# A four-layer stack on one core: order of loads, bias rows and sums in its first stage

## The reference, cut to what matters

```python
x = x + L0_xattn(layernorm(x), ctx, W, b)     # the first stage
x = x + L0_ffn(layernorm(x), Wg, W1, W2, W3)  # 8 experts, each takes its 512 best rows
x = x + L1_xattn(layernorm(x), ctx, ctx, mask, W_out)
x = x + L1_ffn(layernorm(x), w_gate, w_up, w_down)

def L0_xattn(x1, x2, W, b):
    W1, W2 = W[:, :256], W[:, 256:]
    part1 = einsum('bld,ed->ble', x1, W1)
    part2 = einsum('bld,ed->be', x2, W2) / 154
    return part1 + part2[:, None, :] + b

def layernorm(x):
    return (x - mean(x)) / sqrt(var(x) + 1e-5)
```

## Time and profile before

| what | value |
|---|---|
| median of 3 executions | 898.93 us (898.59 to 900.31) |
| the profiled execution, its own time | 899.15 us |
| its span in the trace | 897.4 us |
| first stage (this block) | 0 to about 78.5 us |
| busy in the whole span: PE / DVE / ACT / POOL | 688.7 / 684.1 / 499.9 / 210.8 us |
| granted TensorE clock, mean | 0.87 of full |

### The profile page before, as it was taken

How to read it: one execution, slowest core, us unless ns; L and a number is a source line. 1 busy time by engine, 2 the same in 40 slices (tenths; PEclk the granted TensorE clock), 3 DMA queues, 4 the chain that set the end, 5 groups by cost and what they waited for, 6 DMA issues and landing times.

```text
span 897.4 us, 11482 instructions
## 1 busy us (share of the span) xinstructions
PE 688.7 (77%) x3995; PEld 529.0 (59%) x3995; DVE 684.1 (76%) x1379; ACT 499.9 (56%) x624; POOL 210.8 (23%) x169
## 2 busy tenths in 40 slices
PE   4794227399999954899999999987999995002998
PEld 3573215388988842446665666556887873002998
DVE  5798782378667728999878786887888999997564
ACT  1031010354334432668688786765556997995873
POOL 4621500426656743210111101002430000000000
PEclk9897555599999995899999999998999997555999
DMA  9445620335563456001003100012311732101343
GB/s 325 172 151 187 213 86 3 106 108 124 125 185 60 62 100 222 1 1 43 25 1 128 33 24 25 8 41 95 141 47 37 247 138 93 47 0 47 95 132 104
DMA packets 59491, 84.89 MB, mean 95 GB/s; under 512 B 7984, under 2 KB 47536, under 8 KB 57904
## 3 DMA queue, kind: packets, MB, share of 16 engines
q1 hardware_dynamic: 50176, 61.30, 20.6%
q0 software_dynamic: 7872, 21.11, 9.7%
q10 hardware_dynamic: 1392, 1.82, 0.6%
HBM read 53.68 MB, written 30.54 MB: 94 GB/s over the span
## 4 chain that ended last, share of the span: by engine, by line
PE 45%; DVE 17%; ACT 7%; issue 5%; POOL 4%; DMA 3%; DVEq 0%; ACTq 0%; POOLq 0%
PE bank L1888 8%; PE bank L1844 7%; PE bank L2077 5%; PE bank L2089 4%; PE bank L1313 4%; PE bank L1347 3%; DVE peak L1617 3%; PE bank L1403 3%; PE bank L1370 3%; PE bank L1367 3%; PE bank L1328 2%; POOL x_dram L1934 2%; ACT wgateT L1779 2%; DVE qx L1120 2%; DMA x_dram<-wdownT,idx 1%
## 5 line engine op out<-in xcount | busy, mean ns | idle before, releaser
L1209 ACT ACTIVATE x<-bank,bic 128x512 f32<-128x512 f32 x160 | 105.6, 691 | 38.0 <-PE bank L1347 35.5
L1120 DVE TENSOR_REDUCE qx<-bank 128x4 fp32r<-128x616 f32 x128 | 98.1, 796 | 23.4 <-PE bank L1313 21.8
L1844 PE MATMUL bank<-ux,uwh 128*128 128x512 f32 x384 | 98.5, 395 | 2.6 <-ACT ux L1745 2.4
L1844 PEld LDWEIGHTS bank<-ux,uwh 128*128 128x128 f32 x384 | 71.8, 190 | 20.7 <-issue 3.5
L1347 PE MATMUL bank<-qT,K 128*128 128x512 f32 x128 | 62.6, 500 | 4.2 <-ACT x L1209 1.7
L1313 PE MATMUL bank<-Kb,qTb 128*128 128x308 bf16 x256 | 56.3, 313 | 7.4 <-DVE qx L1120 3.0
L2038 ACT ACTIVATE wgateT<-bank 128x512 f32<-128x512 f32 x32 | 19.1, 597 | 72.8 <-PE bank L2077 72.2
L1834 PE MATMUL bank<-cst,amax 128*1 128x128 f32 x6 | 1.6, 329 | 70.3 <-DVE amax L1589 70.3
L2077 PE MATMUL bank<-xh,wh 128*128 128x512 f32 x128 | 50.8, 397 | 4.7 <-DVE xl L1956 4.7
L1844 PE MATMUL bank<-ux,uwl 128*128 128x512 f32 x192 | 52.2, 394 | 0.0
L2077 PE MATMUL bank<-xh,wl 128*128 128x512 f32 x128 | 50.5, 394 | 0.0
(11 more groups left out here) (352 smaller groups left out, 2023.8 us busy)
## 6 DMA issues: line engine op xcount, KB each, us to landing
xs_dram<-ux POOLq DMA_DIRECT2D x6, 1024.0 KB, 4.2
ux<-xs_dram POOLq DMA_DIRECT2D x6, 1024.0 KB, 5.6
x_dram<-x SPq DMA_DIRECT2D x4, 1024.0 KB, 5.3
xr<-in_w1T SPq DMA_DIRECT2D x8, 512.0 KB, 3.8
xr<-in_w3T SPq DMA_DIRECT2D x8, 512.0 KB, 4.7
xr<-in_w2T SPq DMA_DIRECT2D x8, 512.0 KB, 6.5
row_dram<-xn SPq DMA_DIRECT2D x8, 512.0 KB, 3.1
xr<-x_dram SPq DMA_DIRECT2D x8, 512.0 KB, 7.5
```

The source lines that it names most:

```text
L1120: dve.tensor_reduce(qx[:, k, g * GH:(g + 1) * GH, MROW].rearrange("p (u h) -> p u h", u=2), pair[i][:].rearrange("p (u x) -> p u x", u=2)[ ...
L1209: act.activation(pr[g % 2][h], S_[u % 2], ACT.Exp, bias=bic[:, s // 2, h // GH:h // GH + 1]).then_inc(p_done, 1)
L1844: mm = pe.matmul(bank[j][:, m * TB:(m + 1) * TB], w[:, c * HI + cols:c * HI + cols + P], x[:, part, c * TB:(c + 1) * TB], start=(w is uwh ...
```

## The change

- SyncE waits for w2_in (wx2T and b have landed) behind `rows(1)`, before all other loads. The mask goes ahead of `rows(3)`, the keys' load ahead of step 4's transposed rows, and step 5's ahead of `rows(4)`.
- ScalarE makes all context sums before the first root, and scales the keys at s = 3 and 4.
- VectorE makes the bias rows of batches 1 to 3 at u = 1 directly behind the additions, and the key remainders at u = 10 and 11.
- GpSimd waits before the bias rows of steps 1, 3, 5 and 7 until the first tile of x1 of the step before is added (s_x1 of 1, 9, 17, 25).
- TensorE makes the bias products of batches 1 to 3 directly behind times_w1(2).

```diff
                     rows(1)
+                    sp.wait_ge(w2_in, 32)
                     turned_rows(1)
                     rows(2)
                     turned_rows(2)
                     turned_rows(3)
-                    rows(3)
                     sp.dma_start(mrow[:], ...)
                     sp.dma_start(mcol[:], a["mcol"]).then_inc(g_mk, 16)
                     sp.dma_start(sel[:], a["sel"]).then_inc(g_mk, 16)
+                    rows(3)
+                    key_loads(sp, raw0, 0)
                     turned_rows(4)
+                    turned_rows(5)
                     rows(4)
-                    turned_rows(5)
                     stored(0)
                     turned_rows(6)
-                    key_loads(sp, raw0, 0)
                     turned_rows(7)
...
                     context_sum(0)
-                    rooted(0)
                     act.wait_ge(ctx_in, 16)
                     for b in range(1, B):
                         context_sum(b)
+                    rooted(0)
...
-                        if s in (4, 5):
+                        if s in (3, 4):
                             act.wait_ge(k_set, 3)
                             act.wait_ge(g_mask, 8)
-                            key_heads(act, raw0, K0, Kr0, 0, s - 4)
+                            key_heads(act, raw0, K0, Kr0, 0, s - 3)
...
                         added(u, 1)
+                        if u == 1:
+                            dve.wait_ge(s_sums, SUM_BIAS + B - 1)
+                            for i in range(1, B):
+                                bias_sum(i)
...
                             refined(b)
-                        if u == 1:
-                            dve.wait_ge(s_sums, SUM_BIAS + B - 1)
-                            for i in range(1, B):
-                                bias_sum(i)
...
-                        if u in (11, 13):
-                            key_remainders(dve, raw0, K0, Kr0, 0, u // 2 - 5)
+                        if u in (10, 11):
+                            key_remainders(dve, raw0, K0, Kr0, 0, u - 10)
...
                     for s in range(1, NS):
+                        if s % 2:
+                            pool.wait_ge(s_x1, UT * 2 * (s - 1) + 1)
                         pool.wait_ge(x_in[part_of(s)], 16)
                         biased_rows(s * STEP, (s + 1) * STEP)
...
                     times_w1(2)
+                    for b in range(1, B):
+                        biased(b)
                     for s in range(1, NS + 1):
...
                         x1_turn(s - 1)
-                        if s == 1:
-                            for b in range(1, B):
-                                biased(b)
```

## The result

| | before | changed |
|---|---|---|
| median | 899.62 us (898.59 to 900.31, 4 executions) | 884.75 us (884.69 to 886.27, 4 executions) |
| ratio | | 0.984, 95% interval 0.9823 to 0.9857 |
| profiled execution, its time / span | 899.15 / 897.4 us | 886.27 / 884.5 us |
| next stage starts | 79.01 us | 65.88 us |
| from there to the end of the span | 818.4 us | 818.6 us |

The next stage starts where SyncE issues that stage's first load. The kernel is faster by 14.9 us between the medians and by 12.9 between the two profiled executions; the first stage is 13.1 us shorter. The forecast was 885.6 us, a gain of 13.35.

A forecast was written before the change was run, and what follows sets the result against it. In the first stage, VectorE's small operations with two SBUF inputs were taken to wait for running GpSimd instructions. Terms -14.05 + 0.7 = -13.35 us gave 885.6 us against the 898.93 median; range 883.2 to 889.4.

The forecast's parts named there:

- Loads held: First stage's load queue: SP waits for w2_in, b_bc lands at 9.4 us against 11.6; -2.2 us for TensorE.
- Bias products early: TensorE, behind the third times_w1: bias rows 1 to 3 start at 20.7, not 28.00; -7.3 us, 2.2 from the landing.
- Context sums first: ScalarE's accumulating copies before the first root: sums end at 14, root wanted at 15.1; cost 0.
- GpSimd held: VectorE's batch 1 chain at u=2 and 3 runs undisturbed: 12.21 us becomes 3.67, -8.5 us.
- Keys earlier: VectorE: second key remainders (1.78 us) now also lie before u=12, which starts at 52.6.
- TensorE at the end: Last transposes at 59.1 against 73.15, -14.05 us; closing variance then waits for GpSimd's key mask, +0.7.
- 1: Rival: b_bc's landing not earlier, or held loads or context late; +2.2, 887.8 us; chance 0.17.
- 2: Rival: VectorE's masks or u=2's chain meet a GpSimd add and wait out its rest; 888.1 us; chance 0.08.
- 3: Rival: TensorE's clock dips after an idle gap, costing some 1.6 us; 887.4 us; chance 0.08.
- 4: Rival: the lock isn't the cause, VectorE's chain stays slow with GpSimd idle; 894.3 us; chance 0.03.
- 5: Rival: slower, TensorE at the 1.2 GHz level from first to last transposes; 912.7 us; chance 0.03.
- 6: Rival: no change, what was gained is waited away in the next stage; chance 0.01.

The follow-up runs named there:

- e3: Changed kernel without the load queue's wait for w2_in: 887.23 us, ratio 0.9883.
- e4: Changed kernel with bias products 1 to 3 back behind the first transposes of x1: 890.6 us, ratio 0.9914.
- e9: Changed kernel with the statistics of tiles 0 and 1 again ahead of the bias rows at u=1: 884.85 us, ratio 0.9851.
- e11: Changed kernel with the first root again ahead of the context sums of batches 1 to 3: 885.39 us, ratio 0.9858.
- e1: Kernel before the change plus only GpSimd's waits on the first x1 tile: 891.03 us, ratio 0.9917.
- e2: Changed kernel without GpSimd's waits: 893.09 us, ratio 0.9937.
- e6: Changed kernel with the key steps back at u=11 and 13 (ScalarE's at s=4 and 5): 887.53 us, ratio 0.9872.
- e7: Changed kernel with GpSimd's adds for tiles 20 to 27 released by the mask step, beside VectorE's one-input operations: 889.04 us, ratio 0.9903.
- e5: Changed kernel without GpSimd's waits and with its adds cut to one tile an instruction: 890.45 us, ratio 0.9915.
- e10: e9 with GpSimd's add for tiles 28 to 31 released by the last key remainders instead of u=12: 885.93 us, ratio 0.9866.
- e8: e9 with mask loads ahead of x, mask steps in VectorE's idle start, and GpSimd's last add released by the last key remainders: 885.12 us, ratio 0.9863.

## Why the prediction was right

The time, 884.75 us, lies 0.85 under the forecast, and the steps held one by one:

- Loads held: first bias product at 9.62, forecast 9.4, and e3 gives the hold 1.9 us for the 2.2 of the sum. The rows for tiles 8 to 15 came at 17.55, with a wait of 0.65 us that the slack took.
- Bias products early: 20.70 for 20.7; without the move (e4) 23.42. The +0.7 for the statistics was there (u=2 at 23.67 for 23.7), and e9 shows that it needn't be paid.
- Context sums first: priced at nothing, and e11 says nothing. They ended at 13.97, forecast 14.
- GpSimd held: -8.5 forecast, 3.67 us in u=2 and 3 as said; e1 shows the hold alone as sufficient for it, and e2 that without the hold the stalls stay. This is the largest term. In e2 it is worth 9.8 us: as in the kernel before five operations of the chain wait out an add, but each has more of it still in front (1.95 us against 1.7 on average).
- Keys earlier: u=12 at 52.72 for 52.6. The prediction booked this step as a cost. It did not say that it also keeps the key remainders clear of the key mask, which is worth about 2.2 us by e6. This is one reason why the parts do not add up, and e2's fallen clock is another: the hold alone took 7.4 us off the stage (e1), all the rest 2.5 (e2), and both together 13.1.
- TensorE at the end: last transposes at 59.38 for 59.1; its idle before u=11's was 2.00 for 1.7. The closing variance waited 0.62 for 0.7.
- Sum: -13.35 forecast for the stage, -13.13 measured. The rest of the medians' 14.9 lies behind the stage, where the two profiled executions differ by only 0.2; it is within the scatter. That the time came within 0.9 us of the forecast is in part luck, since the part behind the stage alone differs by up to 4 us.

Of the rivals, 1 was what e3 brought back. 2 (a meeting on the lock) did not happen: the masks began at 32.83, 0.25 us behind the end of an add. e7 shows what it costs: 4.1 us, with two adds in the way, where the prediction had 2.3 for one. The Trainium skill's rule (SBUF — State Buffer, the lock on the shared port pair) names operations in a two-port mode with one input as well; the rows of before could not show it, and here e5's L444 and e7's L499 agree with it. 3 (the clock) was priced at 1.6 us. It costs that at the last transposes (1.7 by e10), and about 1.0 at the end of the stage, since the wait on the key mask goes. Its chance of 0.08 was far too low: of nine profiled executions with the 2.00 us idle the clock fell in four (e2, e3, e5, e10) and stayed in five, two of them the changed kernel's. The argument for the low chance, that each dip had followed a longer idle, does not hold either, as these four followed 2.00 us. That both profiled executions of the changed kernel were spared is luck. Whether key remainders behind u=11, where TensorE doesn't wait for them, would close the gap was not tried. 4 fell with e1, e2 and e5, 5 and 6 with the result. The times of rivals 2 to 5 were reckoned from the profiled execution (885.8) and not, as the forecast was, from the median (885.6); this changes no reading.

## What to carry to other kernels

When tiny VectorE operations take as long as a GpSimd instruction, look at whether that instruction runs beside them, and place GpSimd's work beside VectorE work that does not wait for it: here additions with one input in PSUM, statistics and reciprocals kept their times beside the adds (e5). Cutting the GpSimd instructions smaller was worth about two thirds of holding them (6.6 us against 3.7, from 13.4). A change that frees an engine makes the next waits visible: here TensorE's idle of 2 us at u=11, behind which its clock falls or not, and a key mask that the closing variance has to wait for. An idle engine at the start of a kernel is not free room if what fills it must be loaded ahead of the first data (e8).

## What the runs showed beyond that

The part behind the first stage, which no kernel here changes, lasted from 816.3 us (e11) to 820.7 (e8) in the profiles. The largest piece of that difference is the last matrix stage, which took 66.4, 67.7 or 70.0 us. Of that, 1.3 us goes with its first 20 us (granted clock 0.92 in the executions with 66.4 us, 0.85 or 0.86 in the others). The other 2.3 us arise at a fully granted clock (1.00 behind the first 20 us in both kernels below). Its matmuls have two paces; the kernel before and then the changed one, in the view of the line:

```profile
L1888 PE MATMUL bank<-uwl,oh x192: 276/276/415, 826.0 to 893.4; 128*128 128x256 f32 x192
```

```profile
L1890 PE MATMUL bank<-uwl,oh x192: 278/281/416, 810.8 to 880.5; 128*128 128x256 f32 x192
```

The changed kernel had 70.0 us in one execution and 66.4 in the other (its second measurement), so it is not the kernel. What sets the pace is open. It means that a stage's own start and end tell parts of 1 us apart where the times of whole executions don't. Even these scatter, by 0.25 us at the last scores and in e6 by 1.1 us at the first loads, so an effect is best read between the milestones just before and behind it.
